# Sums over groups of edges moved to every second step of an expert loop, two at a time

## The chip, the cores and the metric

The kernel runs on one core of a Trainium2 chip. The metric is the device time of one execution in microseconds (us). TensorE (PE) does the matmuls, VectorE (DVE) and ScalarE (ACT) the elementwise work, GpSimd (POOL) issues the indirect gathers, SyncE (SP) issues the plain transfers.

## What is computed

Two layers over a graph of 6250 nodes with 256 features and 106250 edges sorted by destination. Each layer is a graph part followed by a mixture of 8 experts of which 2 are used for each node; every part has a residual and works on a normalised input.

```python
# layer 0
msg = feat[src] * eweight
agg = segment_sum(msg, dst); deg = segment_sum(1, dst)
x  = x + concat([agg / max(deg, 1), feat]) @ W.T + b
x  = x + sum_e combine[:, e] * (relu(x_n @ W1[e] + b1[e]) @ W2[e] + b2[e])   # hidden width 512
# layer 1
h  = relu(x_n @ Wp.T + bp)
agg = sqrt(segment_sum(h[src] ** 2, dst))
x  = x + h @ W1.T + b1 + agg @ W2.T + b2
x  = x + t, then the experts with gelu                                        # hidden width 256
```

(`x_n` is the normalised `x`; in layer 1 the graph part has no edge weight other than `edge_weight`, which multiplies the gathered row.)

## The kernel before

Nodes are cut into 14 tiles: eleven of 512 nodes, then 256, 256 and 128. Edges are cut into 208 groups of 512. As the edges are sorted by destination, a group's destinations fall into a window of 40 columns.

The path of one group. POOL fetches its 512 source rows with 4 indirect DMAs into a ring (`gather_group`, L574): the ring holds 4 groups in layer 0 and 8 in layer 1, and group `g` waits until `group_summed` says that group `g - R` has been used. DVE makes a one-hot matrix and multiplies in the edge weights (`onehots`, L1042 and L1043 in layer 0, L1047 and L1048 in layer 1). PE sums the group into the 40 columns of `psE` (`sum_groups`: 24 matmuls of L636 and 4 of L640 in layer 0, L644 in layer 1; fp32 matmuls count twice in the trace). DVE adds the 40 columns into the accumulator `acc` (`add_windows`, L1072) and reports it in `window_added`. PE's next `sum_groups` waits for that report.

The expert part of a tile is a loop of `M` steps `n`: 8 experts times 4 (layer 0, `M = 32`) or 2 (layer 1, `M = 16`) blocks of 128 hidden columns. In step `n` PE does `up` for step `n + 2` (6 matmuls, L654), every few steps `spread_weights` (L661), then `down` for step `n` (6 matmuls, L675), then the groups that the plan gives to step `n`. ACT applies the activation (L1413) and rounds to fp16 (L1420), DVE multiplies with the expert's weight (L1231) and makes the low part (L1236). After its own two operations in step `n`, DVE adds the windows of step `n - 1` and makes the one-hots for step `n + 1`. Each engine runs its instructions in the order in which they are written, so these places are fixed when the program is built.

While a tile's experts run, the edges of the next tile are summed, and its linear part, normalisation and gate are put between the steps. The plan (`plan`, L346) puts the 17 groups of a full tile into steps: some early, from step 28 (layer 0) or step 1 (layer 1) of the tile before, and the rest late, in steps 0 to 12 (layer 0) or in step 0 (layer 1). `take` (L1074) turns `acc` into the next tile's aggregate; it needs all the tile's windows and stands at step 13 in layer 0 and step 1 in layer 1. The tiles' starts are seen in the trace at L670, the first matmuls of `down(0)`.

Of the kernel before, what the change touches and what calls it, by code (L numbers as in the profile page):

```python
# [65 lines left out]
def build_program(nc, a, n_nodes, n_edges):  # L66
# [51 lines left out]
    with ctx:  # L118
# [142 lines left out]
        class Layer:  # L261
# [84 lines left out]
            def plan(self):  # L346


                steps = [[] for _ in range(self.M * NT + 2)]
                self.begun = [[] for _ in range(4)]  # L350
                for t in range(1, NT):
                    gs = list(sh.groups(t))
                    early = len(gs) * (self.M - self.turn) // self.M
                    late = gs[early:]
                    for k, g in enumerate(gs[:early]):
                        if t == 1:
                            self.begun[k * 4 // early].append(g)
                        else:
                            n = self.turn + k * (self.M - self.turn) // early
                            steps[self.M * (t - 2) + n].append(g)  # L360
                    for k, g in enumerate(late):
                        steps[self.M * (t - 1) + k * self.at_take // len(late)].append(g)
                self.steps = steps

            def at(self, t, n):
# [1221 lines left out]
```

## Time and profile before

| | us |
|---|---|
| median of 3 runs | 3461.74 |
| lowest and highest | 3453.28, 3462.49 |
| the profiled execution's own time | 3481.98 |
| its span in the profile | 3479.6 |
| busy: PE, DVE, ACT, POOL | 2549.6, 1772.1, 1141.7, 1681.7 |

The profiled execution is 0.6% above the median, and 2.4 us lie around its span. PE is busy for 73% of the span, but busy time of PE is modelled from starts of pipelined matmuls, so it is an upper view of its work. No engine is busy throughout: what the time hangs on is read from waits. "remote" as a releaser means that the profile found no instruction on this core that ended the wait, which in a program on one core is a signal whose sender it could not name. "idle before" is the time that an engine did nothing before an instruction.

### The profile page before, as it was taken

What the parts mean: (1) busy time and instruction counts of PE and PEld (TensorE: products, weight loads), DVE (VectorE), ACT (ScalarE), POOL (GpSimd) and SP (SyncE); (2) the same over time, 40 slices, a digit from 0 to 9 for tenths busy, and PEclk for the clock granted to TensorE, in tenths of its full rate; (3) what the DMA queues carried; (4) which work ended last, traced back from release to release, by engine and by line L of the source; (5) the groups of instructions that cost most, each with busy time, mean ns of one, the idle gap of its engine ahead of it and who ended that gap; (6) DMA issues with size and microseconds to landing.
All of it is one profiled execution on the core that took longest, in us unless ns stands there. A gap on an engine that the chain in (4) does not pass through costs nothing.

```text
span 3479.6 us, 47720 instructions
## 1 busy us (share of the span) xinstructions
PE 2549.6 (73%) x17897; PEld 1426.1 (41%) x17897; DVE 1772.1 (51%) x4296; ACT 1141.7 (33%) x1835; POOL 1681.7 (48%) x1678
## 2 busy tenths in 40 slices
PE   0146878878787888878798872347788777888797
PEld 0123434434343444434344652333444443444455
DVE  7463645445464645546465653324544444554565
ACT  3022423333232323323244550113333333333355
POOL 3646253352625345362622106666666666666520
PEclk9988989989898989989899995568988888888999
DMA  5422122221313122131311111212222211222110
GB/s 219 172 73 84 58 83 64 71 79 52 99 51 98 56 79 71 58 96 55 96 45 49 41 71 48 55 42 53 59 60 59 59 51 54 58 60 59 51 35 11
DMA packets 115790, 237.82 MB, mean 68 GB/s; under 512 B 30290, under 2 KB 69580, under 8 KB 115044
## 3 DMA queue, kind: packets, MB, share of 16 engines
q0 software_dynamic: 66560, 163.68, 16.9%
q1 hardware_dynamic: 48996, 71.05, 6.0%
q8 instruction: 143, 2.34, 0.3%
q14 instruction: 91, 0.75, 0.1%
HBM read 208.95 MB, written 25.67 MB: 67 GB/s over the span
## 4 chain that ended last, share of the span: by engine, by line
PE 47%; another core or an unknown queue 17%; DVE 15%; issue 14%; ACT 5%; DMA 1%; POOL 1%; DVEq 0%; ACTq 0%; SPq 0%; POOLq 0%
PE psY L675 17%; PE psH L654 16%; PE psE L636 3%; PE psM L741 3%; PE psE L644 3%; DVE hsc L1236 3%; DVE hid L1231 2%; ACT hid L1413 2%; PE psC L661 1%; ACT hsc L1420 1%; PE psM L691 1%; PE psE L640 1%; DVE wbuf L984 1%; DVE acc L1072 1%
## 5 line engine op out<-in xcount | busy, mean ns | idle before, releaser
L574 POOL DMA_INDIRECT ring<-table,src_s x1664 | 1653.6, 994 | 1601.5 <-PE psE L640 649.3
L675 PE MATMUL psY<-hsc,wbuf 128*128 128x512 f16 (+2 forms) x4032 | 961.8, 377 | 171.8 <-DVE hsc L1236 120.3
L654 PE MATMUL psH<-xnT,wbuf 128*128 128x512 f16 (+2 forms) x4032 | 982.9, 382 | 55.7 <-issue 32.9
L1413 ACT ACTIVATE hid<-psH,b,scl 128x512 f32<-128x512 f32 (+2 forms) x672 | 486.9, 725 | 1586.3 <-PE psH L654 760.7
L1231 DVE TENSOR_TENSOR hid<-hid,psC 128x512 f32<-128x512 f32 (+2 forms) x672 | 416.3, 619 | 553.3 <-ACT hid L1413 395.1
L675 PEld LDWEIGHTS psY<-hsc,wbuf 128*128 128x128 f16 x4032 | 374.7, 102 | 670.9 <-issue 199.8
L1072 DVE TENSOR_TENSOR acc<-acc,psE 128x120 f32 (+1 forms) x416 | 98.5, 237 | 911.6 <-remote 699.6
L654 PEld LDWEIGHTS psH<-xnT,wbuf 128*128 128x128 f16 x4032 | 389.9, 105 | 420.7 <-issue 146.5
L636 PE MATMUL psE<-ohbuf,ring 128*128 128x40 f16 x4992 | 180.0, 185 | 349.9 <-issue 207.3
L1236 DVE TENSOR_TENSOR hsc<-hid,hsc 128x512 f16<-128x512 f32 (+2 forms) x672 | 416.9, 620 | 0.3 <-ACT hsc L1420 0.3
L1420 ACT ACTIVATE hsc<-hid 128x512 f16<-128x512 f32 (+2 forms) x672 | 380.7, 567 | 9.3 <-DVE hid L1231 9.2
L644 PE MATMUL psE<-ohbuf,ring 128*128 128x40 f32 x1664 | 254.8, 311 | 163.8 <-issue 128.8
L644 PEld LDWEIGHTS psE<-ohbuf,ring 128*128 128x128 f32 x1664 | 258.6, 230 | 204.2 <-issue 177.2
L636 PEld LDWEIGHTS psE<-ohbuf,ring 128*128 128x128 f16 x4992 | 164.9, 100 | 407.7 <-issue 381.9
L661 PE MATMUL psC<-cT,spread 24*128 24x512 bf16 (+2 forms) x224 | 85.8, 383 | 64.6 <-DVE hid L1231 26.8
L1425 ACT ACTIVATE wbuf<-wbuf,scl 128x1024 f16<-128x1024 f32 (+1 forms) x32 | 30.0, 937 | 247.3 <-issue 187.3
L1043 DVE TENSOR_TENSOR ohbuf<-ohbuf,wpair 128x320 f16<-128x320 f16 x208 | 102.9, 495 | 7.1
L741 PE MATMUL psM<-gnn_w,aggs 128*128 128x256 f32 x294 | 84.6, 399 | 11.0 <-ACT featT L1387 11.0
L1135 DVE TENSOR_TENSOR res<-psM,xin 128x512 f32<-128x512 f32 (+1 forms) x50 | 34.0, 680 | 110.5 <-PE psM L741 72.3
L741 PE MATMUL psM<-gnn_w,featT 128*128 128x256 f32 x294 | 86.5, 405 | 4.4 <-issue 4.4
L661 PEld LDWEIGHTS psC<-cT,spread 24*128 24x128 bf16 x224 | 20.5, 91 | 160.1 <-issue 96.0
L640 PE MATMUL psE<-ohbuf,ones_h 128*128 128x40 f16 x832 | 61.1, 185 | 28.8 <-issue 28.6
(152 smaller groups left out, 1635.8 us busy)
## 6 DMA issues: line engine op xcount, KB each, us to landing
ring<-table,src_s POOLq DMA_INDIRECT x1664
wbuf<-w_in SPq DMA_DIRECT2D x2, 4096.0 KB, 17.3
wbuf<-x_in SPq DMA_DIRECT2D x7, 896.0 KB, 11.6
table<-ring SPq DMA_DIRECT2D x7, 896.0 KB, 3.6
feat<-table SPq DMA_DIRECT2D x11, 512.0 KB
xin<-x_in SPq DMA_DIRECT2D x11, 512.0 KB
x_d<-x SPq DMA_DIRECT2D x11, 512.0 KB
xin<-x_d SPq DMA_DIRECT2D x11, 512.0 KB
```

Of the source, the lines that this page charges most:

```text
L574: pool.indirect_dma_start(out=l.ring[:, g % l.R, k, :], out_offset=None, in_=l.table, in_offset=bass.IndirectOffsetOnAxis(ap=src_s[:, c:c ...
L636: mm(psE[:, o + h * W:o + (h + 1) * W], l.ring[:, r, k, c:c + P], ohw0[:, q, k, y, :], start=(k == 0 and m == 0), stop=(k == SUB - 1 and m ...
L644: last = mm(psE[:, o:o + W], l.ring[:, r, k, :], ohw1[:, q, k, :], start=(k == 0), stop=(k == SUB - 1))
L654: last = mm(psH[n % 2][:, 0:TT[t]], l.w1(e, i, k, c), x[:, j, k, 0:TT[t]], start=(k == 0 and m == 0), stop=(k == KD - 1 and m == 2))
L661: mm(psC[:, 0:TT[t]], spread[:, e, :], cT[t % 2][0:3 * NX, 0:TT[t]], start=True, stop=True)\
L675: last = mm(psY[d][:, 0:TT[t]], l.w2(e, i, c, d), hsc[n % 2][:, j, 0:TT[t]], start=False, stop=(n == l.M - 1 and m == 2))
L741: last = mm(psM[b][:, (s % 2) * D:(s % 2 + 1) * D], x[:, s * P:(s + 1) * P], w, start=(m == 0), stop=(m == len(parts) - 1))
L1072: tt_(v, v, ps, ALU.add).then_inc(l.window_added, 1)
L1231: tt_(h, h, psC[:, 0:TT[t]], ALU.mult).then_inc(l.hid_scaled, 1)
L1236: tt_(hsc[n % 2][:, 1, 0:TT[t]], hid[n % 4][:, 0:TT[t]], hsc[n % 2][:, 0, 0:TT[t]], ALU.subtract).then_inc(l.hid_lo, 1)
L1413: f(hid[n % 4][:, 0:TT[t]], psH[n % 2][:, 0:TT[t]], (ACT.Relu, ACT.Gelu)[l.i], scale=l.un_up, bias=l.b1[:, n // l.HC, n % l.HC:n % l.HC + ...
L1420: f(hsc[n % 2][:, 0, 0:TT[t]], hid[n % 4][:, 0:TT[t]], ACT.Copy).then_inc(l.hid_hi, 1)
```

## The change

The plan rounds the step numbers. An early group goes to the odd step at or after its old one, a late group to the even step at or before its old one. Nothing else is changed.

```diff
                         else:
-                            n = self.turn + k * (self.M - self.turn) // early
+                            n = (self.turn + k * (self.M - self.turn) // early) | 1
                             steps[self.M * (t - 2) + n].append(g)
                     for k, g in enumerate(late):
-                        steps[self.M * (t - 1) + k * self.at_take // len(late)].append(g)
+                        steps[self.M * (t - 1) + k * self.at_take // len(late) // 2 * 2].append(g)
```

The plan for a tile with 17 groups, worked out from these lines:

```
layer 0, groups in steps 28..31 | 0..12
before  1 0 1 0 | 2 1 1 1 1 1 2 1 1 1 1 1 1
after   0 1 0 1 | 3 0 2 0 2 0 3 0 2 0 2 0 1
layer 1, groups in steps 0..15
before  2 1 1 1 1 1 1 1 1 1 1 1 1 1 1 1
after   2 1 0 2 0 2 0 2 0 2 0 2 0 2 0 2
```

The groups keep their order. Over all tiles the steps with sums go from 167 to 104 in layer 0 and from 164 to 101 in layer 1.

On PE in layer 0, at the start of a full tile's loop (L670 opens `down(0)`), before:

```order
L670 MATMUL psY<-cT,b2s 128x512 x2
L675 MATMUL psY<-hsc,wbuf 128x512 x6
L636 MATMUL psE<-ohbuf,ring 128x40 x24
L640 MATMUL psE<-ohbuf,ones_h 128x40 x4
L636 MATMUL psE<-ohbuf,ring 128x40 x24
L640 MATMUL psE<-ohbuf,ones_h 128x40 x4
L654 MATMUL psH<-xnT,wbuf 128x512 x6
L675 MATMUL psY<-hsc,wbuf 128x512 x6
L686 MATMUL psM<-ident,yT 128x128 x8
L636 MATMUL psE<-ohbuf,ring 128x40 x24
L640 MATMUL psE<-ohbuf,ones_h 128x40 x4
```

and at the same place of the change:

```order
L670 MATMUL psY<-cT,b2s 128x512 x2
L675 MATMUL psY<-hsc,wbuf 128x512 x6
L636 MATMUL psE<-ohbuf,ring 128x40 x24
L640 MATMUL psE<-ohbuf,ones_h 128x40 x4
L636 MATMUL psE<-ohbuf,ring 128x40 x24
L640 MATMUL psE<-ohbuf,ones_h 128x40 x4
L636 MATMUL psE<-ohbuf,ring 128x40 x24
L640 MATMUL psE<-ohbuf,ones_h 128x40 x4
L654 MATMUL psH<-xnT,wbuf 128x512 x6
L675 MATMUL psY<-hsc,wbuf 128x512 x6
L686 MATMUL psM<-ident,yT 128x128 x8
```

The third group's sum has moved from step 1 to step 0, and step 1 has none.

On DVE at the same place, from its low part of step 0 (the first L1236) to that of step 1 and what follows it, before:

```order
L1236 TENSOR_TENSOR hsc<-hid,hsc 128x512
L1042 TENSOR_TENSOR ohbuf<-iota,drel 128x160
L1043 TENSOR_TENSOR ohbuf<-ohbuf,wpair 128x320
L1231 TENSOR_TENSOR hid<-hid,psC 128x512
L1236 TENSOR_TENSOR hsc<-hid,hsc 128x512
L1072 ISA
L1072 TENSOR_TENSOR acc<-acc,psE 128x3x40
L1072 ISA
L1072 TENSOR_TENSOR acc<-acc,psE 128x3x40
L1042 TENSOR_TENSOR ohbuf<-iota,drel 128x160
L1043 TENSOR_TENSOR ohbuf<-ohbuf,wpair 128x320
```

and in the change, from the second of these low parts on:

```order
L1236 TENSOR_TENSOR hsc<-hid,hsc 128x512
L1072 ISA
L1072 TENSOR_TENSOR acc<-acc,psE 128x3x40
L1072 ISA
L1072 TENSOR_TENSOR acc<-acc,psE 128x3x40
L1056 TENSOR_LOAD base_i
L1072 ISA
L1072 TENSOR_TENSOR acc<-acc,psE 128x3x40
L1042 TENSOR_TENSOR ohbuf<-iota,drel 128x160
L1043 TENSOR_TENSOR ohbuf<-ohbuf,wpair 128x320
L1042 TENSOR_TENSOR ohbuf<-iota,drel 128x160
L1043 TENSOR_TENSOR ohbuf<-ohbuf,wpair 128x320
```

Three windows are added and two groups' one-hots made in one place; the steps beside it have none.

On PE in layer 1, across the start of a tile's loop, before:

```order
L675 MATMUL psY<-hsc,wbuf 128x512 x6
L644 MATMUL psE<-ohbuf,ring 128x40 x4
L654 MATMUL psH<-xnT,wbuf 128x512 x6
L661 MATMUL psC<-cT,spread 128x512
L670 MATMUL psY<-cT,b2s 128x512 x2
L675 MATMUL psY<-hsc,wbuf 128x512 x6
L644 MATMUL psE<-ohbuf,ring 128x40 x8
```

and in the change:

```order
L675 MATMUL psY<-hsc,wbuf 128x512 x6
L644 MATMUL psE<-ohbuf,ring 128x40 x8
L654 MATMUL psH<-xnT,wbuf 128x512 x6
L661 MATMUL psC<-cT,spread 128x512
L670 MATMUL psY<-cT,b2s 128x512 x2
L675 MATMUL psY<-hsc,wbuf 128x512 x6
L644 MATMUL psE<-ohbuf,ring 128x40 x8
```

Step 15 now sums two groups, and step 0 two as before, so the two pairs stand in neighbouring steps there.

## Rows read from the trace of the kernel before

**Rows 1.** The waits: engine, line, waited for; us in total, times, longest.

```profile
ACT hid L1413 <- remote: 747.6, 135, 28.4
DVE acc L1072 <- remote: 699.6, 151, 23.8
PE psY L675 <- DVE hsc L1236: 120.3, 108, 6.3
PE psE L636 <- DMA ring<-table,src_s: 114.5, 3, 103.4
```

**Rows 2.** Timeline of POOL in layer 0: start, length, idle before and releaser.

```profile
1025.34 0.95 POOL L574 DMA_INDIRECT ring<-table,src_s  x1 [1.67 <-PE psE L640]
...
1031.95 0.95 POOL L574 DMA_INDIRECT ring<-table,src_s  x1 [1.87 <-PE psE L640]
...
1059.35 0.95 POOL L574 DMA_INDIRECT ring<-table,src_s  x1 [0.30 <-issue]
1062.65 1.25 POOL L574 DMA_INDIRECT ring<-table,src_s  x1 [2.35 <-remote]
...
1075.12 0.95 POOL L574 DMA_INDIRECT ring<-table,src_s  x1 [2.15 <-PE psE L640]
...
1099.73 1.24 POOL L574 DMA_INDIRECT ring<-table,src_s  x1 [2.40 <-remote]
...
1112.18 1.62 POOL L574 DMA_INDIRECT ring<-table,src_s  x1 [2.44 <-remote]
```

**Rows 3.** Timeline of ACT and DVE at one of these restarts.

```profile
1062.01 0.78 ACT L1413 ACTIVATE hid<-psH,b,scl 128x512 f32<-128x512 f32 x1 [6.81 <-remote]
1062.03 0.28 DVE L1072 TENSOR_TENSOR acc<-acc,psE 128x120 f32 x1 [5.72 <-remote]
```

**Rows 4.** Timeline of DVE's window additions in the same layer-0 tile.

```profile
1032.32 0.28 DVE L1072 TENSOR_TENSOR acc<-acc,psE 128x120 f32 x1 [0.20 <-DVE acc L1072]
...
1075.48 0.28 DVE L1072 TENSOR_TENSOR acc<-acc,psE 128x120 f32 x1 [0.20 <-DVE acc L1072]
1086.70 0.28 DVE L1072 TENSOR_TENSOR acc<-acc,psE 128x120 f32 x1 [7.08 <-remote]
...
1114.21 0.27 DVE L1072 TENSOR_TENSOR acc<-acc,psE 128x120 f32 x1
```

**Rows 5.** Timeline of PE: one sum of a group and the up that follows, at full clock.

```profile
1050.04 0.76 PE L636 MATMUL psE<-ohbuf,ring 128*128 128x40 f16 x24
1050.64 0.25 PE L640 MATMUL psE<-ohbuf,ones_h 128*128 128x40 f16 x4
1050.74 1.46 PE L654 MATMUL psH<-xnT,wbuf 128*128 128x512 f16 x6
```

**Rows 6.** Busy time by stretch: layer 0 with sums, layer 0 without, two layer-1 tiles.

```profile
1031.70:1113.00 81.30, 57.63 (x537) 28.80 (x535) 32.05 (x76) 19.64 (x30) 52.51 (x53) 0.84 0.34 98
1113.00:1171.10 58.10, 55.70 (x306) 28.34 (x304) 39.55 (x78) 24.74 (x39) 7.50 (x8) 0.96 0.14 37
2634.60:2735.10 100.50, 84.85 (x399) 47.37 (x398) 49.53 (x130) 32.15 (x47) 64.82 (x66) 0.81 0.21 57
...
2840.00:2942.40 102.40, 79.62 (x399) 43.92 (x399) 49.24 (x130) 32.70 (x47) 68.49 (x69) 0.86 0.21 56
```

**Rows 7.** Timeline of POOL and DVE in layer 1.

```profile
2742.90 0.94 POOL L574 DMA_INDIRECT ring<-table,src_s  x1 [2.50 <-remote]
...
2761.94 0.95 POOL L574 DMA_INDIRECT ring<-table,src_s  x1 [0.30 <-issue]
2765.82 0.20 DVE L1072 TENSOR_TENSOR acc<-acc,psE 128x40 f32 x1 [9.35 <-remote]
```

**Rows 8.** The page's groups: one-hots and the two DVE operations of a step.

```profile
L1231 DVE TENSOR_TENSOR hid<-hid,psC 128x512 f32<-128x512 f32 (+2 forms) x672 | 416.3, 619 | 553.3 <-ACT hid L1413 395.1
...
L1043 DVE TENSOR_TENSOR ohbuf<-ohbuf,wpair 128x320 f16<-128x320 f16 x208 | 102.9, 495 | 7.1
...
L1042 DVE TENSOR_TENSOR ohbuf<-iota,drel 128x160 f16<-128x160 f32 x208 | 66.8, 321 | 2.6 <-issue 2.2
```

## Prediction

> **What bounds the kernel now.** I read the waits first [rows 1]. ACT stood 747.6 us and DVE 699.6 us waiting for signals with no named sender, at L1413 (which waits for `up`) and at L1072 (which waits for a group's sum). Both can only come from PE. In layer 0 PE itself waited for gathered rows three times (114.5 us, of which 103.4 is the start), so late data is not the limit there. For DVE's `hsc` it waited 120.3 us.
>
> Then I read POOL's timeline in one layer-0 tile [rows 2]. The gathers come in batches. The batch from 1062.65 and the one from 1099.73 hold 8 gathers, two groups; they are followed by the next batch 12.47 and 12.45 us later, and from 1075.12 two batches pass in 24.61 us. A gather is 0.95 us with 0.30 us before it, so 8 take 10.0 us, and 2.4 us are left between batches. A batch of `b` groups therefore costs `5.0 b + 2.4` us. The reader is to see what ends these pauses: POOL's last gather before one starts at 1059.35 and ends at 1060.3, and at 1062.01 and 1062.03 ACT and DVE start together after 6.81 and 5.72 us of idleness [rows 3], POOL 0.6 us after them. Three engines that wait for different signals of PE are let go within 0.02 us of each other, some 1.7 us after the last gather of a batch has been issued. PE's own rows say that a sum takes little: 24 matmuls in 0.76 us and 4 in 0.25 us, then `up` at 1.46 us (1.3 start to start) [rows 5]. So I take it that a sum that PE starts while gathers are in flight is not reported until they have landed, and that what stands behind it in PE is not reported either. I call this the hold. What causes it no row shows; that it is there, these rows do. It makes a lock: POOL waits for the sum, the sum's signal waits for POOL's batch.
>
> The lock explains the stretches [rows 6]. In layer 0 the phase with sums takes 81.3 us, with PE busy 57.63 and POOL 52.51; the phase without sums, 58.1 us, has PE busy for 55.70. In layer 1 two tiles take 100.5 and 102.4 us, of which 17 groups of gathers need 85.0; the rest is 17 us, or about 7 pauses of 2.4 for 17 groups.
>
> **What the change does, part by part.**
>
> *Work.* The numbers of matmuls, gathers, one-hots and additions stay. Nothing is removed from any engine, so a gain must come from waits.
>
> *Layer 0, where the steps with one sum are now steps with two or three.* A pair is already in the kernel before: step 0 and step 6 sum two groups. After the pair of step 6 (its second addition at 1075.48) the next addition comes at 1086.70, 11.2 us later [rows 4], and POOL's batch for the pair is one of the two in the 24.61 us above. So a pair costs 12.4 us like two singles: with singles the first goes through at once after a restart and the second is held. In the phase with sums I count: before, from the second addition of step 0 (1032.32) to that of step 12's sum (1114.21), 13 groups in 81.9 us. In the change the bursts at steps 2, 4, 6, 8, 10 and 12 are each preceded by the gathers that the burst before them allowed: 3, 2, 2, 3, 2, 2 groups. That is 14 x 5.0 + 6 x 2.4 = 84.4 us, 2.5 more for the same steps. The burst of step 0 also comes later. Before, POOL restarts for step 30's sum at 1025.34 and for step 0's at 1031.95, 6.6 us apart, two steps. In the change step 31's sum comes one step of 2.8 us later than step 30's did (two steps of 1.3 + 1.3 us, with `spread_weights`), and only one step lies between it and the burst of three, which therefore meets a batch in flight and is held for 5.0 + 2.4 = 7.4 us instead of 6.6. That is 2.8 + 0.8 = 3.6 us, of which I count 2.9, since the restart for step 0's first sum in before is 0.7 ahead of its second. The last sum stands in step 12 before and after, so nothing comes back behind it. Sum: 2.5 + 2.9 = 5.4 us a tile, 54 us for ten full tiles and about 3 for the short ones, **+57 us if every burst is held to the end of its batch**. The other bound: if holds end inside a batch, as they do in layer 1, where one batch of 16 gathers lasts from 2742.90 to past 2761.94 without a pause [rows 7], pauses are saved. Half of the six each tile is 10 x 7.2 = 72 us back, -15 us. Between -15 and +57 the locked end is nearer to the rows of layer 0, where seven pauses for 13 groups (13 x 5.0 + 7 x 2.4 = 81.8) give the measured 81.9. I take **+30 us**, one pause of the six saved (57 - 24 = 33).
>
> *Layer 1.* If each burst is locked, 17 groups are 8.5 pairs of 12.4 us, 105.4 us for a tile. The tiles take 100.5 and 102.4 now, so the full lock would be 3 to 5 us a tile slower; over nine full tiles **+31 us** (by 3.4, against a mean of 102.0 that lies between these two rows). With pauses as often as now it is 0. I take a third of it, **+10 us**, since a pair is on PE for longer than a single and is more likely to meet a gather.
>
> *DVE.* After a burst of three, DVE has three additions (0.28 us, 0.48 from start to start), two one-hots (0.32 + 0.50 each) and then one multiplication and one low part (0.62 each) [rows 3, 8]: 1.4 + 1.6 + 1.3 = 4.3 us. PE has `up`, `down`, `up` to do meanwhile, 3.9 us at full clock [rows 5]. So 0.4 us can be bare, but the next burst is held to 12.4 us after the last anyway, which hides it. If the hold were gone, it would cost 0.4 us at 20 places, 8 us.
>
> *`take` and the queue of PE.* `take` stands in step 13 behind the addition of step 12's sum, as before; a later sum makes it later by the same time, which the 5.4 us hold already. What the change frees is the wait for `window_added`: PE finds it done a step earlier. It is no gain, since under the hold the signals of `up` are held as well, and ACT and DVE stand still.
>
> *Clock.* The granted clock is 0.84 in the phase with sums and 0.96 in the phase without [rows 6], that is, PE falls from 2.4 to 1.2 GHz for part of it, after it has stood idle in a hold. Per pair the idle time stays in one piece of the same length, so I cost it at nothing. The Trainium skill (Perfetto Trace Analysis, Matmul Optimizations) speaks for the change here: it says that PE's power follows its use, so that matmuls should run back to back in batches. By that rule longer bursts would lift the clock. Were it 0.96 in this phase, PE's 57.63 us would fall by 0.84/0.96 to 50.4. The trace of before can't tell, as every burst in it is one or two groups.
>
> The sum: 30 + 10 = +40 us on the profiled execution's 3481.98 us (2.4 of them around the span), 3522. That execution is 0.6% above the median of 3461.74, so against the median the same sum is 3461.74 + 40 = 3501. The discount in layer 0 stops at one saved pause a tile where half was the bound; two saved would make the sum 24 less. I round towards that, to **3495 us**.
>
> **The rivals.**
>
> *Fewer holds.* The hold might be a matter of each meeting of a sum with a gather, not a lock. There are 205 steps with sums instead of 331. If POOL then ran through, a layer-0 phase would be 13 x 5.0 + 2.4 = 67.4 instead of 81.9 us, and a layer-1 tile 87.4 instead of 102: 10 x 14.5 + 9 x 14.6 = 276 us, 3186 us. Half the pauses saved gives about 3380 (6.5 pauses of 2.4 for 19 tiles, halved, is 74 to 80 us). For it: the batch of 16 gathers in [rows 7]. Against it: the pair of step 6, followed by a full 11.2 us. Chance 0.25, for anything from 3360 to 3450. A gain could also come from the clock: 57.63 us of PE at 0.84 are 50.4 us at 0.96, 7 us for each of ten phases, 3390 us, if the holds end sooner with it; 0.03 of the 0.25 is for that.
>
> *The full lock.* Every burst is held, in both layers: +57 + 31 = 88 us, 3550 us. It decides where a sum that starts 3 us or more into a batch never gets through. Against it is only [rows 7]. Chance 0.17.
>
> *Nothing moves.* The pauses stay as many as they are in both layers, and the later burst of step 0 is swallowed by a hold that ends sooner: 3462 us, within 10 us. For it: equal cost of pairs and singles at 12.4 us. Chance 0.2.
>
> The forecast, 3472 to 3525, has 0.38.
>
> **How the numbers follow.** A measurement of this kernel can tell about 0.3%, 10 us. Slower by more than that: 0.38 + 0.17 = 0.55, less 0.03 for a forecast that is met at its low edge, 0.52. Same: 0.2. Faster: 0.28, the first rival and that edge's far side. The range should leave out 2 in 10: it goes from 3400, into the first rival (0.12 left below), to 3545, just short of the full lock (0.08 above).
>
> **What would show it.** In the new profile POOL's batches in the phase with sums are 8 and 12 gathers, restarts follow each other at 12.4 and 17.4 us, DVE adds two or three windows in a row 0.4 to 0.5 us apart, the phase from the burst of step 0 to that of step 12 takes 84 us, and a layer-0 tile is 3 to 5 us longer. The "remote" waits of L1413 and L1072 stay near 1450 us together. I am wrong if restarts are fewer than bursts (many batches of 16 and more: first rival), or if PE's wait for `hsc` [rows 1] grows far over 120 us, which would make DVE's heap of work after a burst the new limit.

## Result, and the profile after

The changed kernel takes 3582.11 us (median of 4 runs, 3568.62 to 3586.85) where the kernel before takes 3460.18 (4 runs): ratio 1.0335, interval 1.0308 to 1.0362. It is slower, as forecast, but by 3.35% (the medians stand 122 us apart) and not by 33 us, and it lies above the range of the forecast.

One thing must be known to read the numbers below. The runs fall into six groups, and each lists the kernel before beside it. In five groups that took 3460 to 3486 us; in one, that of e13, e14, e15 and e17, on another chip of the same kind, 2979 us. So ratios are compared across groups, and times only inside one.

First the page of the kernel after: busy times, then the granted clock in tenths over 40 slices.

```profile
PE 2584.2 (72%) x17897; PEld 1458.2 (41%) x17897; DVE 1777.8 (50%) x4296; ACT 1137.7 (32%) x1835; POOL 1664.0 (47%) x1678
...
PEclk9988988989898988989899985567887788778899
```

The waits of the kernel after, which answer to [rows 1]:

```profile
ACT hid L1413 <- PE psH L654: 986.6, 419, 13.1
ACT hid L1413 <- remote: 515.4, 69, 27.1
DVE acc L1072 <- remote: 470.9, 70, 22.8
PEld psY L675 <- DVE hsc L1236: 322.2, 241, 15.0
PE psY L675 <- DVE hsc L1236: 229.2, 133, 13.3
POOL ring L574 <- PE psE L644: 198.6, 59, 12.3
PE psE L636 <- DMA ring<-table,src_s: 109.0, 3, 103.9
```

The waits without a named sender fell by 461 us together, and the time rose. But the named waits for PE at the same two lines rose by 419 us (for `up` from 760.7 to 986.6, for sums from 189.9 to 383.3), so most of this is another label on the same idle time, and it is no measure of the loss. What grew is PE's wait for `hsc`: 120.3 to 229.2 us for the matmuls [rows 1], 197.4 to 322.2 for the weight loads, which stand in the same gaps.

The windows below hold nine full tiles of layer 0 and nine of layer 1 (length; busy time of PE, PEld, DVE, ACT and POOL; granted clock; DMA share; GB/s). Of the kernel before:

```profile
409.80:1789.30 1379.50, 1141.90 (x8775) 576.76 (x8776) 727.36 (x1589) 461.24 (x721) 613.93 (x610) 0.90 0.25 72
2426.80:3325.80 899.00, 709.98 (x3527) 390.22 (x3526) 436.72 (x1147) 293.20 (x415) 576.47 (x586) 0.85 0.21 56
```

Of the kernel after:

```profile
411.40:1835.70 1424.30, 1168.60 (x8776) 594.38 (x8775) 730.75 (x1590) 458.28 (x721) 602.05 (x612) 0.89 0.24 70
2466.70:3422.90 956.20, 714.69 (x3528) 401.91 (x3528) 438.89 (x1147) 293.19 (x415) 575.92 (x589) 0.83 0.20 53
```

A layer-0 tile went from 153.3 to 158.3 us, a layer-1 tile from 99.9 to 106.2: 102 us for the eighteen, against 97 us between the two spans.

The two layers lose in different ways. In the layer-1 window PE's wait for `hsc` at L675 goes from 45.5 to 151.4 us. In the layer-0 window it stays (28.9 and 26.1 us), and PE's wait at L661 for DVE's `scale` goes from 3.4 to 41.4.

The pattern on POOL is near the forecast one. POOL's timeline in a layer-0 tile of the kernel after, only gathers that end a pause of over 1 us:

```profile
1222.00 0.95 POOL L574 DMA_INDIRECT ring<-table,src_s  x1 [2.57 <-remote]
...
1229.93 0.94 POOL L574 DMA_INDIRECT ring<-table,src_s  x1 [3.12 <-PE psE L640]
...
1242.21 0.94 POOL L574 DMA_INDIRECT ring<-table,src_s  x1 [2.29 <-PE psE L640]
1245.20 0.94 POOL L574 DMA_INDIRECT ring<-table,src_s  x1 [2.05 <-issue]
...
1255.88 0.94 POOL L574 DMA_INDIRECT ring<-table,src_s  x1 [1.93 <-PE psE L640]
...
1273.68 0.94 POOL L574 DMA_INDIRECT ring<-table,src_s  x1 [2.92 <-PE psE L640]
```

The restarts stand 7.9, 12.3, 13.7 and 17.8 us apart, for one, two, two and three groups; the gap at 1245.20 lies inside a batch and lengthens the 13.7.

### The profile page after: what moved, and what is told of

The parts are those of the page before. It is cut to its first block, busy times and chain, and to the rows that moved or that the text cites. A ratio compares the mean times of both kernels' runs of the same rounds, so it can differ in the third digit from the quotient of the medians.

```text
span 3576.9 us, 47720 instructions
## 1 busy us (share of the span) xinstructions
PE 2584.2 (72%) x17897; PEld 1458.2 (41%) x17897; DVE 1777.8 (50%) x4296; ACT 1137.7 (32%) x1835; POOL 1664.0 (47%) x1678
## 4 chain that ended last, share of the span: by engine, by line
PE 44%; another core or an unknown queue 17%; DVE 17%; issue 13%; ACT 6%; DMA 1%; POOL 1%; DVEq 0%; ACTq 0%; SPq 0%; POOLq 0%
PE psY L675 16%; PE psH L654 14%; PE psE L644 4%; PE psM L741 3%; PE psE L636 3%; DVE hid L1231 3%; DVE hsc L1236 3%; ACT hid L1413 2%; PE psC L661 1%; ACT hsc L1420 1%; DVE acc L1072 1%; PE psM L691 1%; ACT L1413 1%; DVE wbuf L984 1%
## 5 line engine op out<-in xcount | busy, mean ns | idle before, releaser
L574 POOL DMA_INDIRECT ring<-table,src_s x1664 | 1635.9, 983 | 1719.3 <-PE psE L640 777.7
L675 PE MATMUL psY<-hsc,wbuf 128*128 128x512 f16 (+2 forms) x4032 | 970.1, 380 | 252.8 <-DVE hsc L1236 229.2
L1413 ACT ACTIVATE hid<-psH,b,scl 128x512 f32<-128x512 f32 (+2 forms) x672 | 485.8, 723 | 1601.7 <-PE psH L654 986.6
L1231 DVE TENSOR_TENSOR hid<-hid,psC 128x512 f32<-128x512 f32 (+2 forms) x672 | 415.5, 618 | 624.0 <-ACT hid L1413 474.6
L675 PEld LDWEIGHTS psY<-hsc,wbuf 128*128 128x128 f16 x4032 | 376.0, 103 | 754.8 <-DVE hsc L1236 322.2
L636 PE MATMUL psE<-ohbuf,ring 128*128 128x40 f16 x4992 | 203.9, 185 | 339.0 <-issue 193.1
L1236 DVE TENSOR_TENSOR hsc<-hid,hsc 128x512 f16<-128x512 f32 (+2 forms) x672 | 415.7, 619 | 0.3 <-ACT hsc L1420 0.3
L636 PEld LDWEIGHTS psE<-ohbuf,ring 128*128 128x128 f16 x4992 | 174.8, 100 | 390.2 <-issue 350.8
L661 PE MATMUL psC<-cT,spread 24*128 24x512 bf16 (+2 forms) x224 | 85.6, 382 | 95.5 <-DVE hid L1231 56.9
L661 PEld LDWEIGHTS psC<-cT,spread 24*128 24x128 bf16 x224 | 20.5, 91 | 189.0 <-issue 108.1
```

The costliest lines, as they stand in the source:

```text
L574: pool.indirect_dma_start(out=l.ring[:, g % l.R, k, :], out_offset=None, in_=l.table, in_offset=bass.IndirectOffsetOnAxis(ap=src_s[:, c:c ...
L636: mm(psE[:, o + h * W:o + (h + 1) * W], l.ring[:, r, k, c:c + P], ohw0[:, q, k, y, :], start=(k == 0 and m == 0), stop=(k == SUB - 1 and m ...
L661: mm(psC[:, 0:TT[t]], spread[:, e, :], cT[t % 2][0:3 * NX, 0:TT[t]], start=True, stop=True)\
L675: last = mm(psY[d][:, 0:TT[t]], l.w2(e, i, c, d), hsc[n % 2][:, j, 0:TT[t]], start=False, stop=(n == l.M - 1 and m == 2))
L1231: tt_(h, h, psC[:, 0:TT[t]], ALU.mult).then_inc(l.hid_scaled, 1)
L1236: tt_(hsc[n % 2][:, 1, 0:TT[t]], hid[n % 4][:, 0:TT[t]], hsc[n % 2][:, 0, 0:TT[t]], ALU.subtract).then_inc(l.hid_lo, 1)
```

## Experiments

**One layer at a time (e1, e2).**

```diff
# e1; e2 has  | self.i  and  // (1 + self.i) * (1 + self.i)
-n = (self.turn + k * (self.M - self.turn) // early) | 1
+n = (...) | (1 - self.i)
-... // len(late) // 2 * 2
+... // len(late) // (2 - self.i) * (2 - self.i)
```

> The rounding in layer 0 alone; layer 1 keeps the plan of before. Lock theory (a sum begun while gathers are in flight is reported only when they have landed, a batch of b groups costs 5.0 b + 2.4 us): layer-0 tiles 158.3 us as in the whole change, about 46 us above before, 3505 us; layer-1 tiles 102. Rival (VectorE's heap of additions and one-hots behind a burst makes PE wait for hsc): about the same total, but then the loss must show as PE's wait for hsc, some 50 us more than the 120 of before.

> The rounding in layer 1 alone. Both theories: about 60 us above before, 3520 us, the two halves adding up to the whole change. Lock theory: layer-1 tiles near 105 us by 8.5 pairs of 12.4; 107.8 as in the whole change would be more than the lock gives. Rival: PE's wait for hsc 60 us above before.

e1 took 3504.34 us, ratio 1.0120 (1.0085 to 1.0156); e2 3526.67, ratio 1.0193 (1.0151 to 1.0234). Together 3.1%, near the whole 3.35%. Each layer loses by itself, layer 1 more: there the forecast had 10 us, and 60 were lost by the medians. PE's wait for `hsc` at L675, in e1 and then in e2:

```profile
PE psY L675 <- DVE hsc L1236: 108.9, 111, 8.3
```

```profile
PE psY L675 <- DVE hsc L1236: 210.0, 115, 10.9
```

In e1 the lock theory had its time (3505 us) and, within 1 us, its tile (157.4), and the rival did not have its sign: the wait for `hsc` is below the 120.3 us of before, where some 170 were asked. e2's wait is 90 us above before, as the rival wanted, and its tile of 105.8 us is near the 105 of the lock.

**Without most gathers (e3, e4).** The suspect was the hold, so the gathers were cut to a quarter under both plans.

```diff
-for k in range(SUB):
+for k in range(SUB if g < l.R else 1):
...
-pe.wait_ge(l.gathered[g % l.R], 16 * SUB * (g // l.R + 1))
+pe.wait_ge(l.gathered[g % l.R], 16 * (SUB + g // l.R))
```

> The kernel before, but once the ring has been filled only the first of a group's four gathers is issued; the other three quarters of the rows in the ring are old ones, so the sums are over wrong rows, while every matmul, one-hot and addition stays. Lock theory: a batch then lasts 1.3 to 2.5 us instead of 5 to 10, the holds shrink, a layer-0 tile falls from 153 to under 138 us and a layer-1 tile from 102 to under 85, 3100 to 3200 us in all. Rival (the stalls are PE's and VectorE's own): 3400 us or more.

> The same with the changed plan (three quarters of the gathers left out, old rows summed in their place). Lock theory: with short batches singles and pairs cost the same, within 25 us of the run of before with a quarter of the gathers. Rival (heap on VectorE): 80 to 120 us above it, as the pile of additions and one-hots is unchanged.

e3 took 2610.55 us (ratio 0.7539), e4 2720.58 (0.7857). Two things follow. The gathers cost the kernel before some 850 us, the time to issue them included. And the change costs 110 us with a quarter of them, in total about what it costs with all; whether it is the same loss is looked at further down. The windows of e3, then of e4:

```profile
333.60:1357.40 1023.80, 1013.22 (x8774) 550.12 (x8774) 726.61 (x1589) 460.25 (x721) 172.07 (x152) 1.00 0.13 39
1844.70:2456.30 611.60, 588.59 (x3527) 352.42 (x3526) 433.98 (x1147) 291.71 (x415) 146.84 (x147) 1.00 0.12 35
```

```profile
338.80:1409.30 1070.50, 1023.13 (x8776) 549.12 (x8775) 724.57 (x1590) 462.07 (x721) 152.88 (x153) 1.00 0.12 37
1898.60:2564.70 666.10, 606.61 (x3527) 354.58 (x3526) 436.44 (x1147) 293.09 (x415) 145.97 (x147) 0.98 0.11 33
```

PE stood idle for 10.6 us of layer 0's nine tiles in e3 and for 47.4 in e4, in layer 1 for 23.0 and 59.5. Where, the steps say. From the traces of these two kernels, and of e7 below, the time from the first matmul of `down` in one step to that of the next, mean over nine layer-0 tiles, steps 0 to 12:

```
step   0    1    2    3    4    5    6    7    8    9   10   11   12   sum
e3   4.0  4.6  4.0  3.3  3.3  3.7  4.9  3.3  3.3  5.4  3.3  3.7  3.3  50.1
e4   4.7  5.2  4.3  3.4  4.0  3.4  5.6  5.0  4.3  4.7  4.0  3.0  3.3  54.9
e7   4.7  3.9  5.7  2.6  4.0  3.0  5.6  3.6  4.0  4.7  4.0  3.0  3.3  52.1
```

Without waits a sum is 0.7 us and a bare step 2.6. In e4 the loss stands in steps 1, 3 and 7, steps without a sum behind a burst, where e7 has 3.9, 2.6 and 3.6. The timeline of e4 at steps 1 and 2:

```profile
938.03 0.78 ACT L1413 ACTIVATE hid<-psH,b,scl 128x512 f32<-128x512 f32 x1 [4.70 <-PE psH L654]
938.05 0.28 DVE L1072 TENSOR_TENSOR acc<-acc,psE 128x120 f32 x1 [3.92 <-remote]
...
939.13 1.46 PE L654 MATMUL psH<-xnT,wbuf 128*128 128x512 f16 x6
939.32 0.32 DVE L1042 TENSOR_TENSOR ohbuf<-iota,drel 128x160 f16<-128x160 f32 x1
...
940.43 0.49 DVE L1043 TENSOR_TENSOR ohbuf<-ohbuf,wpair 128x320 f16<-128x320 f16 x1
...
940.84 0.68 DVE L1231 TENSOR_TENSOR hid<-hid,psC 128x512 f32<-128x512 f32 x1
...
941.58 0.39 PE L661 MATMUL psC<-cT,spread 24*128 24x512 bf16 x1 [0.99 <-DVE hid L1231]
...
942.18 1.47 PE L675 MATMUL psY<-hsc,wbuf 128*128 128x512 f16 x6 [0.21 <-DVE hsc L1236]
```

The reader sees DVE's heap (three additions, two pairs of one-hots, 938.05 to 940.9) ahead of `scale` at L1231, though ACT had given it its `hid` by 938.8. PE, which has only one `up` (and the transposes of step 1) to do meanwhile, stands for 0.99 us ahead of L661 and 0.21 ahead of L675.

**The one-hots moved out of the heap (e5, e6, e7), and a heap made under the old plan (e8, e12).**

```diff
# e5: on the changed plan; e6: on the plan before; e7: as e5, a quarter of the gathers
-onehots(l, l.at(t, n + 1))
+onehots(l, l.at(t, n))
# the call for the first step, ahead of the loop, goes; in e8 and e12 it makes steps 0 and 1
# e8: on the plan before; e12: as e8, a quarter of the gathers
-onehots(l, l.at(t, n + 1))
+if n % 2:
+    onehots(l, l.at(t, n + 1) + l.at(t, n + 2))
```

> The changed plan (TensorE's part is the same row for row), but VectorE makes the one-hot matrices of a burst in the burst's own step, behind that step's hidden_low, instead of one step ahead in one heap with the additions of the burst before. The heap of a step falls from three additions and three pairs of one-hots (4.3 us) to 1.9 us of additions in one step and 2.4 us of one-hots in the next. Theory A (the loss of 117 us is TensorE and ScalarE waiting for scale and hidden_low behind VectorE's heap): most of it comes back, 3460 to 3510 us, and TensorE's idle time that ends with VectorE's hsc at line 1236 falls from 551 us towards the 318 of before. Theory B (TensorE's own burst of 2 to 3 sums is what starves the chain up, activation, scale, low part, down, whatever VectorE does): 3570 to 3595 us. Theory C (the hold of TensorE's reports while gathers are in flight, longer after a longer burst): 3570 to 3595 us too, with hsc's idle time little changed.

> The kernel before with the same move of the one-hot matrices into the step of their own sum: VectorE has per step hidden_low, one addition, one pair of one-hots either way, only the pair is made a step later. Theory A: the heap before is 1.4 us in every step and stays so, so the time is that of the kernel before within 15 us (3445 to 3475). If TensorE is made to wait for the one-hots instead (0.8 us behind hidden_low, while down takes 1.3 us, so it should not), up to 208 groups x 2 layers x 0.3 us = 125 us slower: 3480 to 3580.

> The changed plan with the one-hot matrices in their own step, and with only one of a group's four gathers made once the ring has been filled (three quarters of the gathered rows are stale, so the sums are not the reference's). To be held against 2610.6 us (plan before, a quarter of the gathers) and 2720.6 us (changed plan, a quarter). Theory A: 2610 to 2650 us, TensorE's windows of a layer-0 tile back from 118.8 towards 113.8 us and of a layer-1 tile from 75.1 towards 68.5. Theories B and C: 2710 to 2730 us.

> The kernel before with TensorE's order kept (one group a step), but VectorE makes the one-hot matrices of two steps together at every second step: heaps of 0.6 + 1.6 = 2.3 us and 0.6 us in turn, instead of 1.4 us in each. Theory A: part of the loss comes, since a step's heap is now as in the changed plan's bursts of two without their second addition; 3475 to 3530 us. Theories B and C (TensorE's bursts): nothing changes, 3450 to 3475 us.

> The plan before with a quarter of the gathers (stale rows as in e3) and the one-hot matrices of two steps made together at every second step, as in e8. To be held against 2610.6 us. Theory A (a heap alone is enough to make TensorE wait): 2625 to 2660 us. If a heap costs only when TensorE has no sum to do in the step behind it, as in the changed plan: 2605 to 2620 us.

e7 took 2648.28 us: moving DVE's one-hots by one step took back 72 of e4's 110 us, with PE's order the same row for row. The timeline of e7 at the same place as e4's above:

```profile
919.02 0.28 DVE L1072 TENSOR_TENSOR acc<-acc,psE 128x120 f32 x1 [0.20 <-issue]
919.22 0.68 DVE L1231 TENSOR_TENSOR hid<-hid,psC 128x512 f32<-128x512 f32 x1
...
920.34 0.38 PE L661 MATMUL psC<-cT,spread 24*128 24x512 bf16 x1
...
920.66 1.47 PE L675 MATMUL psY<-hsc,wbuf 128*128 128x512 f16 x6
```

L1231 follows the third addition at once, and PE's L661 and L675 have no wait. So theory A holds for two thirds of the loss where gathers are few (three quarters, if each run is taken as a ratio to its own group's kernel before: 0.7857, 0.7612 and 0.7539 for e4, e7 and e3). With all gathers e5 took 3551.35 us, ratio 1.022 (1.0185 to 1.0256): the same move took back only a third, and the 3460 to 3510 us of A was missed, as were the 3570 to 3595 of B and C. e6 (3490.84 us, ratio 1.0038, 1.0016 to 1.0060) shows that the move is no gain by itself; beside e6, in the same group and with the same order on DVE, e5 is 60 us slower.

e8 (3488.54 us, ratio 1.0024) and e12 (2597.33 us against e3's 2610.55) go against theory A as it was written: a heap of two pairs of one-hots costs 8 us in the one and nothing in the other, while PE has a sum in nearly every step. With few gathers, then, heap and bare step must come together, and the change makes both with one rounding.

**The additions apart too (e9, e10).** A burst's first addition stays, the others go one step later, behind `hidden_low`:

```diff
-add_windows(l, l.at(t, n - 1))
+owed += l.at(t, n - 1)
+k = len(owed) if l.at(t, n) or n == l.at_take else 1
+add_windows(l, owed[:k], owed)
+owed = owed[k:]
```

> The changed plan with a quarter of the gathers (three quarters of the gathered rows are stale, so the sums are not the reference's), the one-hot matrices in their own step as in e7, and of a burst's additions only the first in the step behind the burst: the others follow one step later, behind that step's scale and hidden_low and ahead of the next burst, which TensorE's six down products hide. To be held against 2610.6 us (plan before), 2720.6 (changed plan) and 2648.3 (one-hots moved). Theory A (what is left of the loss is the heap of additions): 2610 to 2630 us. Theory B (what is left is TensorE's own burst, which makes the up product of the step behind it late for ScalarE): 2640 to 2655 us.

> The same two moves in VectorE's order with all gathers made, so a complete computation. Ratio to the kernel before: 1.034 for the changed plan, 1.022 with the one-hots moved. Theory A alone: 1.00 to 1.01. Theory B: 1.02. Theory C (longer holds behind a burst that is begun with gathers in flight, which a quarter of the gathers had taken away): 1.015 to 1.025, whatever e9 shows.

e9 took 2643.99 us, 4 less than e7; e10 3572.74, ratio 1.0231 (1.0205 to 1.0258), no better than e5 and inside the 1.015 to 1.025 of theory C. The additions aren't the rest; e9 lies where its theory B (PE's own burst) had it. What is left in e7 and e9, 33 to 38 us, has two marks. Step 2 takes 5.7 us, where the one-hots now lie ahead of `result` (L1245, L1251 and L1116, 3.1 us of DVE). And late reports are still there. The DVE waits of e3, then of e9:

```profile
DVE acc L1072 <- remote: 21.7, 2, 13.8
```

```profile
DVE acc L1072 <- remote: 88.7, 20, 14.6
```

POOL's and PE's timeline in e4 shows how a burst makes one of these waits for itself:

```profile
934.16 0.25 PE L640 MATMUL psE<-ohbuf,ones_h 128*128 128x40 f16 x4
...
934.96 0.76 PE L636 MATMUL psE<-ohbuf,ring 128*128 128x40 f16 x24
935.17 0.94 POOL L574 DMA_INDIRECT ring<-table,src_s  x1 [2.40 <-PE psE L640]
...
936.42 0.95 POOL L574 DMA_INDIRECT ring<-table,src_s  x1 [0.31 <-issue]
```

The burst's first sum frees a slot, POOL starts a gather at 935.17 while PE is in the third sum (934.96 to 935.8), and DVE hears of the third only at 938.05, 0.7 us after the second gather's 937.37. A single sum has no second sum behind it to be caught. How much of the 33 us is this and how much `result` was not taken apart.

**With all gathers, step by step.** The same reckoning for the runs with all gathers, means over nine tiles of each layer, in us. For layer 0: when DVE adds the last window of step 0's sums and of step 12's, from the tile's first `down`; what follows to the next tile; the tile. For layer 1: steps 0 to 3, the other twelve, the tile.

```
                              layer 0                  layer 1
                              step 0  step 12  behind  tile    0..3  others  tile
before                           4.0     86.4    66.9  153.3    27.2    72.7   99.9
e8   before, one-hots paired     4.0     87.0    66.2  153.2    26.5    74.4  100.9
e6   before, one-hots moved      3.9     87.8    68.3  156.1    26.1    73.6   99.7
after                           18.1     90.6    67.7  158.3    32.6    73.6  106.2
e18  after, again               18.1     90.8    66.7  157.5    35.4    69.2  104.6
e5   after, one-hots moved      14.4     90.4    64.6  155.1    33.2    70.6  103.8
e10  and additions apart        17.7     91.0    63.8  154.8    33.7    75.8  109.5
```

The loss with all gathers is not the loss of e4 over again. In layer 0 the last sum comes 4 us later under the changed plan, 90.4 to 91.0 us after the tile's start, and DVE's order does not move it: there the pace of the gathers sets the time, and the heap is hidden. What e5 and e10 take back stands behind the last sum, where no burst is left; why, these runs don't say. In layer 1 the loss stands in steps 0 to 3, where the two pairs of steps 15 and 0 and the single sum of step 1 are followed by a bare step 2, and DVE's order does not move it either. The timeline of the kernel after at such a step 2:

```profile
2474.39 1.47 PE L654 MATMUL psH<-xnT,wbuf 128*128 128x512 f16 x6
...
2480.06 0.38 PE L654 MATMUL psH<-xnT,wbuf 128*128 128x512 f16 x1 [1.31 <-issue]
...
2484.65 0.94 POOL L574 DMA_INDIRECT ring<-table,src_s  x1 [0.30 <-issue]
...
2488.61 0.78 ACT L1413 ACTIVATE hid<-psH,b,scl 128x512 f32<-128x512 f32 x1 [12.47 <-remote]
2488.64 0.20 DVE L1072 TENSOR_TENSOR acc<-acc,psE 128x40 f32 x1 [14.15 <-remote]
...
2492.99 0.68 DVE L1236 TENSOR_TENSOR hsc<-hid,hsc 128x512 f16<-128x512 f32 x1
...
2493.73 2.74 PE L675 MATMUL psY<-hsc,wbuf 128*128 128x512 f16 x6 [13.30 <-DVE hsc L1236]
```

The wait of 13.30 us is put down to `hsc`. But the `up` of 2474.39 had ended by 2475.9, and ACT was let go only at 2488.61, with DVE, 3.0 us after POOL's last gather of the batch. PE had stood since 2480.4: 8.2 us of its wait lie ahead of this report, and 5.1 behind it, with the heap, `result` (L1245), `biased` (L1110) and `scale` on DVE. Of PE's waits for `hsc` in step 2 of the nine tiles (45.2 us, against 1.6 before) five make 42.0, and ahead of each ACT had stood for 7.6 to 12.5 us. So a large part of what the profile calls a wait for `hsc` in layer 1 is a late report.

**The sums of layer 0 over more steps (e11, e13, e16), and the change on top (e14).** Steps 0 to 12 hold nearly the whole cost of the gathers in layer 0: reckoned as in the first table of steps they take 85.3 us in the kernel before, and 50.1 in e3.

```diff
# e11 on the plan before; e13: 18 in place of 20; e14: 20, changed plan; e16: 18, RING = [5, 10]
-self.turn = (28, 1)[i]
+self.turn = (20, 1)[i]
```

> The kernel before with layer 0's turn at step 20 in place of 28: of the 17 groups of a tile, 6 (in place of 2) are summed in steps 20 to 30 of the tile before, and 11 (in place of 15) in steps 0 to 12, so that fewer steps of 0 to 12 hold a sum begun while gathers are in flight, and the gathers are spread over more of a tile. Theory C (TensorE waits because its sums in steps 0 to 12 are paced by the gathers, 6.2 us a group): a layer-0 tile falls from 153 to 135 to 148 us, and the time to 3280 to 3430 us. If each sum costs its hold wherever it stands: 3440 to 3480 us.

> The kernel before with layer 0's turn at step 18 (7 groups of a tile early, 10 late), where turn 20 (6 early, 11 late) gave 3300 us and a layer-0 tile of 136.4 us against 153.3. If each group moved out of steps 0 to 12 saves as those before it did (17 us for 4 groups, so 4.2 us each): 132 us a tile, 3255 us. If the transformer's other work in steps 18 to 19 (a step of 6.1 and one of 6.0 us in every kernel) and the gathers' own pace take it: 3290 to 3320 us.

> The changed plan with layer 0's turn at step 20, to be held against e11's ratio of 0.947. If the change costs what it did (1.034): 0.979 to 0.985, 3405 to 3430 us. If its cost in layer 0 was bound to the crowded steps 0 to 12: 0.965 to 0.972.

> The kernel before with layer 0's turn at step 18 and a ring of 5 groups in layer 0 and 10 in layer 1. Turn 18 alone gave a ratio of 0.958 where no reports come late, and turn 20 0.947 where they do. If the pace of the gathers no longer binds layer 0 (a tile of 114.7 us, the 113.8 of a quarter of the gathers): the ring gives nothing, 0.955 to 0.960 without late reports. With late reports: 0.930 to 0.950, the ring being worth up to one prefetched group a tile, 5 us.

e11 took 3299.85 us, ratio **0.9472** (0.9445 to 0.9500): a complete computation, faster than both kernels, with a layer-0 tile of 136.4 us. e16 took 3279.25, ratio 0.9464 (0.9427 to 0.9501), so turn 18 and the larger ring add nothing that shows in the ratio, though the layer-0 tile of its profile is 131.6 us. On the other chip e13 took 2856.19, ratio 0.9583 (0.9565 to 0.9601), and e14 2862.40, ratio 0.9610 (0.9592 to 0.9629): there the changed plan, with its bursts in layer 0 now of one and two and all of its heap, stands 0.2% above e13, whose turn is two steps earlier. e14's expectation started from the other ratio and can't be judged by it.

**Layer 1's rest (e15, e17, e18).** e15 is e2 with `onehots(l, l.at(t, n + 1 - l.i))`, e17 adds a ring of 10 groups in layer 1, e18 is the changed kernel again.

> The change in layer 1 alone (as e2, ratio 1.019), with layer 1's one-hots made in their own step. If the heap of one-hots were layer 1's whole loss: 1.000 to 1.005. As the tiles of e5 have it (99.9, 106.2, 103.8 us): 1.010 to 1.013, with GpSimd's wait for a summed group of layer 1 at 140 to 210 us, against 53 before.

> As e15, with a ring of 10 groups in layer 1 in place of 8, so that GpSimd can run two groups further ahead of a burst. Theory P (the rest of layer 1's loss is GpSimd idle behind a burst, since a layer-1 tile's 68 gathers take 85 of its 100 us): 1.000 to 1.006, GpSimd's wait for layer 1's sums well under e15's. Theory C (the sums' reports are late because gathers are in flight, whoever waits): the same as e15 within 0.4%, or slower, as more gathers are in flight at once.

> The changed kernel itself, once more. If the chip shows no late reports (the kernel before at about 2980 us): layer 1 is bound by its gathers (86 us a tile), which leave room for VectorE's heaps, and only layer 0's 5 us a tile stay: +50 to +60 us, ratio 1.017 to 1.020. If the heap still costs layer 1 its 6 us a tile as well: 1.035 to 1.04. If the chip shows late reports (3460 to 3490 us before): 1.030 to 1.037, as measured.

e15 took 2973.17 us, ratio 0.9975 (0.9960 to 0.9989); e17 2971.63, ratio 0.9981 (0.9971 to 0.9991). Both fell on the other chip, on which no row of any engine waits for an unnamed sender. The windows of layer 1's nine tiles in e13 (plan before), then in e14 (changed plan with its heap):

```profile
1923.10:2706.70 783.60, 654.45 (x3528) 366.85 (x3528) 437.69 (x1147) 291.64 (x415) 600.74 (x601) 0.92 0.25 66
```

```profile
1936.50:2707.50 771.00, 665.58 (x3527) 386.88 (x3526) 440.62 (x1147) 294.38 (x415) 587.86 (x602) 0.91 0.25 67
```

A tile takes 87.1 and 85.7 us, and its 68 gathers at 1.25 us are 85. With no late reports POOL is layer 1's limit, and neither bursts nor heap cost it anything. e18 fell on a chip with late reports: 3563.93 us, ratio 1.0299 (1.0256 to 1.0341), the result again. So there is no time of the changed kernel itself on the chip without them.

## Why the prediction was wrong

**The direction** was right. Slower had 0.52.

**The step that failed** is the one on layer 1, "With pauses as often as now it is 0. I take a third of it, +10 us". Its nine tiles took 57 us more, and e2 alone 60 us by the medians, twice even the +31 us of the full lock. The term knew one way to lose, a pause of 2.4 us on POOL for each burst. The runs show two others. One is DVE's heap, which has a price in the prediction only for the bursts of three of layer 0; layer 1 has eight bursts of two in a tile. With a quarter of the gathers layer 1 lost 54.5 us, and the one-hots in their own step took back 34.7 of them (666.10 to 631.40). The other shows only with all gathers: 5.4 us a tile in steps 0 to 3 (27.2 to 32.6), at the two neighbouring pairs and the bare step 2 behind them, which stayed with the one-hots moved (33.2 in e5, 33.7 in e10), with PE waiting behind late reports of `up` and POOL's wait for a group's sum up from 53.3 to 198.6 us. On the chip without late reports it is gone (87.1 us a tile under the plan before, 85.7 under the changed one). By which path a pair makes reports later, the runs don't settle, and how much of the 57 us is the heap stays open.

**DVE.** "0.4 us can be bare, but the next burst is held to 12.4 us after the last anyway, which hides it", "8 us if the hold were gone". With the hold nearly gone it was 72 of 110 us, over both layers. The heap was set against `up`, `down`, `up` as if it began with the last matmul of the burst, but in e4 it began at 938.05, over 2 us after the last sum's end; the first `up` and nearly all of `down` had been used up by then. That the hold hides it was right for steps 0 to 12 of layer 0 with all gathers: the last sum comes at 90.6 us with the heap and at 90.4 and 91.0 without. It was not applied to layer 1, which had no such term.

**Layer 0** came out near its size by luck. Of the full lock's 5.4 us a tile, 2.5 were to lie between the bursts of steps 0 and 12 and 2.9 ahead of them. Measured, the burst of step 0 was added 14.1 us later (18.1 against 4.0), and the stretch from there to step 12's sum was 9.9 us shorter (72.5 against 82.4, where 84.4 was forecast): 4.2 us of the tile's 5.0. The burst of three did not meet one group's batch but three groups' gathers, from 1203.92 on with no gap over 0.74 us; its sums were added after the last of them:

```profile
1218.48 0.95 POOL L574 DMA_INDIRECT ring<-table,src_s  x1 [0.30 <-issue]
1221.38 0.28 DVE L1072 TENSOR_TENSOR acc<-acc,psE 128x120 f32 x1 [14.78 <-remote]
```

The discount from +57 to +30 us, one saved pause a tile, was not there in sum: the nine tiles took 45 us more. That a tile pays 5.0 us with all gathers and 5.2 with a quarter is chance too, since the two losses stand in different steps.

**The hold** is real. The chip without late reports runs the kernel before 480 to 507 us faster; the 850 us of e3 hold the gathers' own time as well. The batch rule, 5.0 us a group and 2.4 a pause, fits: restarts at 7.9, 12.3, 13.7 and 17.8 us where it gives 7.4, 12.4, 12.4 and 17.4. One reading of [rows 3] was too strong: two engines, ACT and DVE, are let go within 0.02 us, and POOL 0.6 us later. The unnamed waits did not stay near 1450 us but fell to 986, for the most part by label.

**The clock.** Costed at nothing, and PE's busy time rose by 27 us in the nine layer-0 tiles and 5 in layer 1's, the granted clock going from 0.90 to 0.89 and from 0.85 to 0.83: a small term that was left out. The Trainium skill's advice to batch matmuls (Perfetto Trace Analysis, Matmul Optimizations) did not raise the clock here. In e3 and e4, where PE seldom stands, it is 0.98 to 1.00 under either plan.

**The rivals.** Fewer holds: POOL's unnamed waits did fall, from 127 (282.2 us) to 55 (120.1), but its named waits for sums rose by more than that, so nothing came of it. Its sum has a slip: 6.5 pauses of 2.4 us for 19 tiles, halved, are 148 us and not 74 to 80, which would have made it some 3310 us. The full lock at 3550 us was nearest in time; it holds for layer 0 in the rough, and its +31 us for layer 1 was half of what came. The condition named at the end, a wait for `hsc` far over 120 us, came true; it had been given no chance and no price of its own, and it stands for two things, the heap and late reports.

## What to carry to other kernels

When work is bunched on one engine, look at the engine that prepares and clears it: its work is bunched into the same step, ahead of whatever stands behind it in its queue, and it meets the steps that the bunching has emptied. Price that heap in every stage, from when it can start, not from when its cause ended. A large wait in a profile (here 850 us of gathers) shows where a gain may lie, as e11's 5.3% does, not what a change near it will cost. Cutting the wait away under both versions shows what else the change costs; it does not show that this is what the change costs while the wait is there. Here the two totals are 110 and 122 us, and only times step by step tell that they are different losses. And where an engine stands for an input, look at what that input's own maker waited for.

## What the runs showed of the hardware

The same kernel took 3460 to 3486 us in five groups of runs and 2979 us in one on another chip, with the granted clock at 0.94 in place of 0.87. The four profiles from that chip (e13, e14, e15, e17) have no waits for an unnamed sender, and the gathers run almost without gaps (layer-1 tile 87.1 us in e13 against 99.9). So the hold is not fixed by the program; what makes it on one chip and not on another was not found. Where it exists, one late report can cover several things that PE has finished: ACT's `up` and DVE's sum were let go within 0.02 us of each other in e4 (938.03 and 938.05) and within 0.03 in the kernel after (2488.61 and 2488.64).
